# A GpSimd product made ahead in its own buffer, twelve zero matmuls between two transforms, and a new order written out by hand

## The reference, cut to what matters

```
x_dct  = DCT over h and w of the normed x (over its second axis, 64 values)
h1     = gelu(conv1x1(x_dct, c1a));  h1 = gelu(depthwise3x3(h1, c1b))
x_conv = h1 + x_dct
h2     = gelu(conv1x1(x_conv, c2))
x_high = h2 + x_conv
x_out  = coef * x_low + (1 - coef) * x_high + x_dct
x      = x + IDCT over w and h of x_out
```

## Time and profile before

| | |
|---|---|
| time, median of 3 runs | 211.08 us (210.69 to 211.94) |
| profiled execution, its own time | 211.93 us |
| its span, first to last instruction | 209.9 us |
| instructions | 5812 |
| TensorE busy | 190.3 us, 91% of the span |
| VectorE, ScalarE, GpSimd busy | 125.2, 122.2 and 44.5 us |
| granted TensorE clock, mean | 0.989 of 2.4 GHz |

### The profile page before, as it was taken

One profiled execution on the slowest core, in us unless ns is written; L12 is line 12 of the kernel. 1 busy time (PEld: TensorE's weight loads), 2 busy tenths in 40 slices (PEclk: granted clock), 3 DMA queues, 4 the chain that ended last, 5 costly groups with the idle time before them and its releaser, 6 DMA issues.

```text
span 209.9 us, 5812 instructions
## 1 busy us (share of the span) xinstructions
PE 190.3 (91%) x2542; PEld 97.4 (46%) x2542; DVE 125.2 (60%) x237; ACT 122.2 (58%) x206; POOL 44.5 (21%) x49
## 2 busy tenths in 40 slices
PE   7387789969687998999999999999999999999992
PEld 2274753447486332344655444354444453444430
DVE  0645659199498999775554799822533515535354
ACT  2255120386423258988566679678777595584840
POOL 5292960402920061069000050000000000000000
PEclk9969999999999999999999999999999999999998
DMA  6992000000000000294035008153036071091001
GB/s 205 268 279 60 6 3 3 0 5 3 0 8 3 3 0 0 69 243 103 3 94 109 3 2 199 54 141 75 0 100 153 0 178 27 0 210 39 3 0 50
DMA packets 6744, 14.17 MB, mean 68 GB/s; under 512 B 2752, under 2 KB 4288, under 8 KB 5824
## 3 DMA queue, kind: packets, MB, share of 16 engines
q1 hardware_dynamic: 6720, 13.81, 26.8%
HBM read 12.63 MB, written 1.18 MB: 66 GB/s over the span
## 4 chain that ended last, share of the span: by engine, by line
PE 84%; ACT 6%; DVE 6%; issue 2%; POOL 0%; DVEq 0%; POOLq 0%
PE psum L738 27%; PE psum L723 27%; PE psum L582 8%; PE psum L460 4%; PE psum L593 2%; PE psum L453 2%; PE psum L603 2%; PE psum L646 2%; PE psum L535 1%; PE psum L614 1%; PE psum L523 1%; ACT h_pad L776 1%; DVE wide L1013 1%; PE psum L555 1%; PE psum L635 1%
## 5 line engine op out<-in xcount | busy, mean ns | idle before, releaser
L723 PE MATMUL psum<-tok,w1s 128*64 128x512 f16 x512 | 62.6, 380 | 0.6 <-ACT hid L868 0.6
L1173 DVE SCALAR_TENSOR_TENSOR term<-psum,sm,wide 128x512 f32<-128x512 f32 x32 | 24.0, 749 | 47.3 <-PE psum L738 46.3
L868 ACT ACTIVATE hid<-psum,b1p 128x512 f32<-128x512 f32 x64 | 39.5, 692 | 19.2 <-PE psum L723 18.4
L723 PEld LDWEIGHTS psum<-tok,w1s 128*64 128x64 f16 x512 | 28.5, 110 | 41.6 <-issue 14.0
L738 PE MATMUL psum<-hid,w 128*64 128x512 f32 x128 | 31.2, 595 | 0.0
L1178 DVE TENSOR_TENSOR x<-x,term 128x512 f32<-128x512 f32 x32 | 24.5, 764 | 1.1
L868 ACT ACTIVATE w1g<-psum,b1p 128x512 f32<-128x512 f32 x32 | 20.0, 699 | 7.0 <-PE psum L723 7.0
L868 ACT ACTIVATE w1f<-psum,b1p 128x512 f32<-128x512 f32 x32 | 20.1, 702 | 4.9 <-PE psum L723 4.8
L582 PE MATMUL psum<-h_pad,tap_bd 64*64 64x512 f32 x144 | 17.2, 610 | 0.7 <-issue 0.7
L738 PE MATMUL psum<-w1f,w 128*64 128x512 f32 x64 | 16.0, 595 | 0.0
L738 PE MATMUL psum<-w1g,w 128*64 128x512 f32 x64 | 15.9, 595 | 0.0
(11 more groups left out here) (141 smaller groups left out, 247.0 us busy)
## 6 DMA issues: line engine op xcount, KB each, us to landing
wide<-gate_store SPq DMA_DIRECT2D x14, 512.0 KB, 6.4
xs<-in_x SPq DMA_DIRECT2D x2, 512.0 KB, 4.1
w1f<-in_W SPq DMA_DIRECT2D x2, 512.0 KB, 9.0
block_out<-x SPq DMA_DIRECT2D x4, 256.0 KB, 6.4
wide<-gate_store SPq DMA_DIRECT2D x2, 384.0 KB, 5.2
hid<-in_W1T SPq DMA_DIRECT2D x1, 512.0 KB, 9.4
w<-in_W SPq DMA_DIRECT2D x1, 512.0 KB, 11.5
c<-const SPq DMA_DIRECT2D x1, 310.0 KB, 6.2
```

What stands on the lines that cost most here:

```text
L723: mm = pe.matmul(h_bank(n)[side * H:(side + 1) * H, :], w1s[:, part, e, k * P + side * H:k * P + (side + 1) * H], tok[:, pair, half, b, :] ...
L868: act.activation(hid_of[u % KEPT][:, B2 * k + b, :], h_bank(n), ACT.Gelu, bias=b1p[:, e * KT + k:e * KT + k + 1]).then_inc(gelu_ready, 1)
L1173: dve.scalar_tensor_tensor(term[:, u % 2, :], y_bank(u), b2t[:, e:e + 1], gate_b[part][:, e % (E // 2), :], ALU.add, ALU.mult).then_inc(te ...
```

## The change

It does four things.

- GpSimd gets a new stage `base(p)` between `join(p)` and `high(p)`. It makes `x_conv * (1 - coef) + x_dct` in a new view `kept`, the second half of `wide[1]` of its pair, in two instructions for each half. `high` then has two instructions for each half instead of three: `h2 * (1 - coef)`, and the sum with `kept`. In all GpSimd has 8 such instructions for a pair where it had 6, of which 4 instead of 6 stand behind the second GELU.
- TensorE gets twelve more zero matmuls behind `dct_over_h(0)`, into a bank that `dct_over_h(1)` writes afterwards.
- `dct_over_h(1)` stands ahead of `dct_over_w(0)` on TensorE. Before it stood behind it.
- The other numbers of `TURN` and `EXPERT_TURN` move: among others `conv_out(0)` ahead of `gram_matrices(1)`, `exponent(0)` ahead of `keep_xt(1)`, `softmax_out(0)` ahead of `mask_gram(1)`, `scale_logits(1)` behind `shares(0)`, `gelu_depthwise(1)` behind `keep_tokens(0)` and `tanh_gap(0)`, `up(0, 0)` ahead of `norms_of_k(1)`, and the places of most `up`s and `down`s.

```diff
-    "dct_over_h": (0, 2), "dct_over_w": (1, 8), "windows": (3, 12), "conv_in": (4, 14), "places": (5, 15),
+    "dct_over_h": (0, 1), "dct_over_w": (2, 8), "windows": (3, 12), "conv_in": (4, 14), "places": (5, 15),
...
-    "weights_of_first": (0, 0), "join": (1, 4), "high": (2, 5), "low_part": (3, 6),
+    "weights_of_first": (0, 0), "join": (1, 5), "base": (2, 6), "high": (3, 7), "low_part": (4, 8),
...
+        kept = [wide[1][:, p, N:2 * N] for p in range(PAIRS)]
...
                     transform(p, j, in_chunks(xs[:, p, :]), dct_h).then_inc(dct_h_done, 1)
+                if p == 0:
+                    hold_clock(12, bank(slot(1, 1), 0))
...
+            def base(p):
+
+                pool.wait_ge(coef_ready, 1)
+                pool.wait_ge(xconv_ready, p + 1)
+                for b in range(B2):
+                    link(pool.tensor_tensor(bank(kept[p], b), bank(x_conv[p], b), coef_rest[:, :], ALU.mult))
+                    link(pool.tensor_tensor(bank(kept[p], b), bank(kept[p], b), bank(xd[p], b), ALU.add))
+
             def high(p):
 
-                pool.wait_ge(coef_ready, 1)
                 for b in range(B2):
                     pool.wait_ge(h2_ready, 2 * p + b + 1)
-                    link(pool.tensor_tensor(bank(h2[p], b), bank(h2[p], b), bank(x_conv[p], b), ALU.add))
                     link(pool.tensor_tensor(bank(h2[p], b), bank(h2[p], b), coef_rest[:, :], ALU.mult))
-                    pool.tensor_tensor(bank(rest[p], b), bank(h2[p], b), bank(xd[p], b), ALU.add).then_inc(rest_ready, 1)
+                    pool.tensor_tensor(bank(rest[p], b), bank(h2[p], b), bank(kept[p], b), ALU.add).then_inc(rest_ready, 1)
```

More of the change, by code:

```diff
@@ L44 @@
 TURN = {
-    "dct_over_h": (0, 2), "dct_over_w": (1, 8), "windows": (3, 12), "conv_in": (4, 14), "places": (5, 15),
-    "gram_matrices": (6, 16), "gram_times_w": (7, 17), "norms": (9, 23), "logits": (10, 25), "taps": (11, 29),
-    "norms_of_k": (13, 31), "conv_out": (18, 42), "project": (19, 44), "heads": (20, 47),
-    "times_wv": (21, 51), "low": (22, 55), "to_frequencies": (24, 59), "inverse_over_kh": (26, 61),
-    "inverse_over_kw": (27, 66), "tokens": (28, 69), "features": (30, 81), "gates_to_rows": (35, 90),
@@ L50 @@
-    "norm_columns": (0, 1), "mask_gram": (2, 9), "products": (3, 11), "inverse_norms": (4, 14),
-    "scale_logits": (5, 16), "biases": (6, 6), "softmax_in": (7, 20), "coefficients": (8, 8),
-    "softmax_out": (10, 21), "mask_mix": (12, 25), "mix_branches": (13, 26), "residual": (15, 29),
-    "norm_tokens": (17, 31), "route": (18, 34), "shares": (19, 37), "square_columns": (0, 2),
-    "keep_dw": (1, 7), "keep_xd": (3, 9), "gelu_in": (4, 10), "keep_xt": (5, 11), "keep_tk": (6, 16),
-    "gelu_depthwise": (8, 21), "exponent": (12, 29), "gelu_out": (13, 31), "keep_y": (14, 33),
@@ L56 @@
-    "keep_yt": (15, 36), "keep_back": (17, 41), "keep_half": (18, 44), "square_tokens": (19, 47),
-    "high_part": (20, 50), "keep_tokens": (22, 54), "tanh_gap": (24, 57), "keep_gates": (27, 59),
-    "weights_of_first": (0, 0), "join": (1, 4), "high": (2, 5), "low_part": (3, 6),
+    "dct_over_h": (0, 1), "dct_over_w": (2, 8), "windows": (3, 12), "conv_in": (4, 14), "places": (5, 15),
+    "gram_matrices": (6, 17), "gram_times_w": (7, 19), "norms": (9, 23), "logits": (10, 25), "taps": (11, 29),
@@ new lines @@
+    "norms_of_k": (13, 32), "conv_out": (16, 38), "project": (18, 47), "heads": (20, 50),
+    "times_wv": (21, 52), "low": (22, 56), "to_frequencies": (24, 60), "inverse_over_kh": (26, 63),
+    "inverse_over_kw": (27, 65), "tokens": (28, 67), "features": (30, 81), "gates_to_rows": (34, 87),
+    "norm_columns": (0, 1), "mask_gram": (2, 10), "products": (3, 11), "inverse_norms": (4, 14),
+    "biases": (5, 5), "scale_logits": (6, 19), "softmax_in": (7, 20), "coefficients": (8, 8),
+    "softmax_out": (9, 22), "mask_mix": (12, 25), "mix_branches": (13, 26), "residual": (15, 28),
@@ new lines @@
+    "norm_tokens": (16, 30), "route": (17, 33), "shares": (18, 36), "square_columns": (0, 2),
+    "keep_dw": (1, 7), "keep_xd": (3, 9), "gelu_in": (4, 10), "keep_xt": (5, 12), "keep_tk": (6, 16),
+    "gelu_depthwise": (8, 23), "exponent": (11, 29), "gelu_out": (13, 33), "keep_y": (14, 34),
+    "keep_yt": (15, 36), "keep_back": (17, 42), "keep_half": (18, 44), "square_tokens": (19, 47),
+    "high_part": (20, 50), "keep_tokens": (21, 55), "tanh_gap": (22, 56), "keep_gates": (26, 58),
+    "weights_of_first": (0, 0), "join": (1, 5), "base": (2, 6), "high": (3, 7), "low_part": (4, 8),
@@ L77 @@
     "add": [
-        22, 23, 24, 27, 28, 30, 32, 33, 35, 36, 38, 39, 40, 41, 42, 43, 44, 45, 46, 47, 48, 49, 50, 51, 52,
+        21, 23, 24, 27, 29, 31, 32, 34, 35, 37, 38, 39, 40, 41, 42, 43, 44, 45, 46, 47, 48, 49, 50, 51, 52,
         53, 54, 55, 56, 57, 58, 59],
@@ L944, in weights_of_first @@
                 pool.tensor_tensor(w1s[:, 1, :, :], w1g[:, :, :], w1s[:, 0, :, :], ALU.subtract).then_inc(w1_ready, 1)
-            for stage, args in in_turn((weights_of_first, join, high, low_part), ()):
+            for stage, args in in_turn((weights_of_first, join, base, high, low_part), ()):
                 stage(*args)
```

## The result

| | before | changed |
|---|---|---|
| median | 210.88 us (210.68 to 211.94, 4 runs) | 214.35 us (213.7 to 216.93, 4 runs) |
| ratio, 95% interval | | 1.0132 [1.0084, 1.0179] |
| profiled execution, its own time | 211.93 us | 214.42 us |
| its span | 209.9 us | 211.8 us |
| instructions | 5812 | 5843 |

The forecast was 211.2 us, the range 209.5 to 212.4 us; the time lies 1.95 us above the range. Ratios leave disturbed executions out, so that one can differ a little from the quotient of two medians.

What follows compares the result with a forecast made beforehand. TensorE's full stretch from 84.5 us was taken as the bound, so the chain up to `up(1, 1)` decides. Terms -0.95 - 0.5 + 1.45 + 0.1 = +0.1 us gave 211.2 us on the median, range 209.5 to 212.4 us.

Steps and rivals of the forecast that it cites:

- Behind that: 0.1 us lost: After the first experts: `base(1)` beside `softmax_in(1)`, and `down(7, 0)`, `gates_to_rows(1)` nearer VectorE's stages; 0.1 us, bounds 0 and 1.3.
- there are no holes to close: TensorE's full stretch from 84.5 us: busy throughout at full clock, so the change cannot help there; no size.
- no DMA moves in its queue: Full stretch from 84.5 us: the change leaves the DMAs' order in their queues as before; no size.
- It frees the gates 2.0 us earlier, but nothing waits for them here: First experts: VectorE's L1122 no longer meets `join(1)`, gates come 2.0 us earlier, with no gain booked.
- lost at the first experts: From `features(0)` to the end of `up(1, 1)`: `norms_of_k(1)` delays the `up`s, 1.45 us lost, bounds 1.0 to 1.6.
- VectorE waits for GpSimd: Rival: `base(0)` and `base(1)` lock L1067 and L1058 for whole instructions; 213.4 us, halfway 212.3; chance 0.10.
- The front: Everything until `up(1, 1)` ends: -0.95 - 0.5 + 1.45, so TensorE enters the full stretch at the same time as before.
- the term of the softmax: Softmax of pair 0: `to_frequencies(0)` starts 0.5 us earlier; bounds 0.85 us gained to 1.75 us later.
- The start's gain: Start: zero matmuls and `dct_over_h(1)` hidden in the pause, `dct_over_w(0)` at full clock; 0.95 us gained, bounds 0 to 1.4.
- the clock does not come up: Rival at the start: clock stays low during the zeros, `dct_over_w(0)` starts 3.1 us late; 213 us or more; chance 0.04.
- the change doesn't do what it says: Rival at the start: zeros and product are made, but the chain through ScalarE does not move; 212.1 us; chance 0.08.
- I am wrong if TensorE has holes of over 0.5 us in it: Sign in the profile after: such holes in TensorE's full stretch, expected from about 84.5 us, would refute the forecast.

Runs made afterwards that it cites:

- the late load: Changed kernel with its third gate load issued one `add` later, no TensorE instruction touched: 211.66 us, ratio 1.0019.
- the first two experiments: Kernel before, unchanged: 211.29 us; kernel before with twelve zero matmuls and `dct_over_h(1)` ahead of `dct_over_w(0)` only: 211.32 us.
- both of the front alone: Kernel before with the change's start and order at the softmax of pair 0: ratio 0.9936; the same with third gate load later: 209.85 us.
- the two stages are back with `join(1)` waiting: Changed kernel, `norms_of_k(1)` ahead of `up(0, 0)`, `gelu_depthwise(1)` ahead of `keep_tokens(0)`, `join(1)` waiting for `shares(0)`: 213.29 us; with third gate load later 210.45 us.
- one instruction for nine: Changed kernel with GpSimd's nine products of `tap_bd` at the start made as one instruction: 214.15 us, ratio 1.0119.

## Why the prediction was wrong

**The failed step is "Behind that: 0.1 us lost"**, and under it the sentences that there are no holes to close and that no DMA moves in its queue. Both are true of the program's text and miss the point: DMAs kept their order, but TensorE's dense stages moved onto one. I read the full stretch as proof that nothing but TensorE's work counts in it. It was a balance of the instruction fetch as well, with 60 matmul records in the last 4 us of the load, where the fetch was held up too and TensorE still shows no hole. The hole and what hangs on it cost 2.1 us (the late load: 123.56 to 121.48 us), against a term of 0.1 with an upper bound of 1.3 for another mechanism. That 1.70 us of it are the hole itself is in the rows; the remaining 0.4 us no row separates.

**The bound of one term was in the wrong place.** "It frees the gates 2.0 us earlier, but nothing waits for them here" holds for the changed kernel. But I booked the 1.1 us lost at the first experts as a cost without a purpose. Put back, they cost 4 to 5 us more (ratio 1.0334 against 1.0132, medians 219.16 and 214.35 us), since `base(1)` then locks VectorE. I had the lock as a rival, "VectorE waits for GpSimd", at the softmax, where it stayed small: L1076 takes 0.87 and 0.69 us, 0.18 us above its own time where I had priced 0.3. For `base(1)`, 30 us later, I had looked at the instructions of `softmax_in(1)` alone, beside which it stands in the new order, and not at `route(0)`, from which that order keeps it away.

**The front came out near its sum, in part by luck.** By the profiled executions:

| step | predicted | measured |
|---|---|---|
| `conv_in(0)` | 15.4, gain 0.95 | 15.61, gain 0.70, with the input landing 0.5 us later |
| gain by `features(0)` | 1.45 | 75.93 - 74.74 = 1.19 |
| L1086, now L1095 | 0.69 | 0.69 |
| lost at the first experts | 1.45 | 9.53 - 8.45 = 1.08 |
| end of `up(1, 1)` | about 84.5 | 84.43 |

The term of the first experts was 0.4 us too large: `gelu_depthwise(1)` ended at 77.33 + 1.09 = 78.42 us, 3.68 behind `features(0)` instead of 3.95, since ScalarE's instructions overlap there, and the rest is in the steps after it.

The row of `features(0)` hides that the term of the softmax failed at the place where it was booked. VectorE kept it: it ends `mix_branches(0)` at 59.27 us instead of 60.87, 1.60 us earlier, of which 0.7 come from the start. But TensorE had a hole by "issue" of 0.96 us just there, before the last matmul of `norms(1)`, so `to_frequencies(0)` starts at 60.23 instead of 60.92, only the start's 0.7 us earlier. First the changed kernel, then the kernel before, which had its hole 5 us later:

```profile
58.58 0.69 DVE L1095 TENSOR_TENSOR place<-place 128x512 f32<-128x512 f32 x1
60.03 0.27 PE L558 MATMUL psum<-wide,c 64*64 64x64 f32 x1 [0.96 <-issue]
```

```profile
60.18 0.69 DVE L1086 TENSOR_TENSOR place<-place 128x512 f32<-128x512 f32 x1
65.70 0.63 PE L460 MATMUL psum<-c,place 64*64 64x64 f32 x28 [0.67 <-issue]
```

That later hole is gone in the changed kernel, so the way from `to_frequencies(0)` to `features(0)` is 14.51 us instead of 15.01; this is the 0.5 us in the table. It hangs on the execution: in the second profile of the kernel before that way takes 14.46 us. Both holes end 1.3 us behind a q8 transfer (58.68 and 64.37 us), here with no load beside it. So the trace of before already held the sign, a stage of small matmuls that stands still for its instructions, and I did not ask what it was.

The start's gain is real in the profiles and small on the median: alone it gives no difference that can be told. The rivals "the clock does not come up" and "the change doesn't do what it says" fell: the granted clock is 1.00 from 9 to 12 us and over the whole execution (mean 0.999). `dct_over_w(0)` did take 1.29 us instead of 1.99. My sentence "I am wrong if TensorE has holes of over 0.5 us in it" names what happened, without a mechanism behind it and without a chance.

**Outside the span** lie 2.6 us in the changed kernel and 2.0 before, which no term of mine had. It is 2.0 in the kernels with the old order (the first two experiments and both of the front alone), 2.4 to 2.6 with the old order and the product, and 2.2 with the new order where the product is gone or the two stages are back with `join(1)` waiting. It does not follow the gate loads' bytes, the zero matmuls' shape, GpSimd's instruction count or its number of waits, nor how many 8 KB instruction transfers (queue q14) start behind the last instruction: one with one instruction for nine (2.5 us outside), two where `join(1)` waits (2.2). What sets it stays open, about 0.6 us of the loss.

The rest, 0.3 to 1.0 us between 2.5 (profiled) and 2.8 to 3.5 us (ratio and medians), is that the profiled execution of before lies above its median, as the prediction noted, and that of after does not.

## What to carry to other kernels

An engine that is busy all the time may still be balanced on its instruction fetch: before stages of many short matmuls are moved closer together, look at what large DMAs run beside them, and issue those where TensorE works through long ones. Before work is moved to GpSimd, list the VectorE instructions with two operands in SBUF beside it in every place where it runs, and ask for each who waits for its chain: here small ones paid up to a whole GpSimd instruction each. And a stage that looks badly placed may be what keeps two engines apart, so undo it alone, and measure, before calling it a loss.

## What the runs showed of the hardware that was not expected

- A load of 1.05 MB that fills the DMA engines (share 0.93 to 1.02) delays TensorE's instruction fetch of 16 KB: its start moved from 111.21 to 114.12 us, 0.23 us before the load's end, and TensorE stood still for 1.70 us. Beside the input's transfers at the start it was 3.22 us. TensorE went on 1.36 us behind the end of the fetch, both times, and 1.2 to 1.6 us behind it in every other hole of the traces. Without a load beside the fetch there were holes too, of 0.67 and 0.96 us.
- Three of VectorE's 128x128 TENSOR_TENSOR instructions with two SBUF operands took 1.05 to 2.32 us beside GpSimd instead of 0.29, a SCALAR_TENSOR_TENSOR 1.17 us likewise, and a reduction among them 0.29.
- Keeping TensorE's clock up through the start (mean 0.99 to 1.00 in ten of twelve executions instead of 0.979 to 0.992) brought nothing on the median that the measurement can tell, ratio 0.9996 [0.9969, 1.0023]. What the clock alone is worth stays open, since that run gave back 0.5 us in the full stretch.
- The profile's windows of before show a granted clock of 1.00 from 1 to 7 us, while its zero matmuls took 0.45 us each, twice the 0.23 us of the twelve later ones in the changed kernel (2.76 us in all). The trace's first record of the clock starts at 7.25 us, so by this trace the 1.00 ahead of it is no measurement, and durations decide there.
